# Value tile 6 moved from the end of the attention opening into the first group's planned order

## The reference

```
x = x + 0.5 * ffn_ref(layernorm(x), ...)      # attention, then a mixture of experts
x = x + attn_ref(layernorm(x), ...)           # RWKV time mix and channel mix
x = x + 0.5 * ffn_ref(layernorm(x), ...)

def attention(x, wq, wk, wv, wo):             # 16 query heads, 4 key/value heads of 128
    q, k, v = x @ wq, x @ wk, x @ wv          # then rotary embedding on q and k
    scores = q @ k.T / sqrt(128), causal
    return softmax(scores) @ v @ wo
def moe(x, gate_w, w1, w3, w2):               # 8 experts, 2 of them per token, softmax of the two logits
```

## Time and profile before

| | |
|---|---|
| time before, median of 3 runs | 1285.56 us (1282.88 to 1286.85) |
| the profiled execution | 1284.35 us, of it 1282.5 us from the first instruction to the last |
| TensorE busy | 1150.7 us, 90% of the span |
| VectorE busy | 951.0 us, 74% |
| ScalarE busy | 783.1 us, 61% |
| GpSimd busy | 600.0 us, 47% |

### The profile page before, as it was taken

The page is one execution under the profiler, slowest core; times in us unless marked ns, Lnnn a source line. Parts: engine busy times, 40 slices in busy tenths (PEclk is TensorE's granted clock), DMA queues, the critical chain, the costliest instruction groups (busy, mean ns, idle before and its releaser), DMA issues.

```text
span 1282.5 us, 18567 instructions
## 1 busy us (share of the span) xinstructions
PE 1150.7 (90%) x6424; PEld 965.5 (75%) x6424; DVE 951.0 (74%) x2013; ACT 783.1 (61%) x1542; POOL 600.0 (47%) x450
## 2 busy tenths in 40 slices
PE   4899999999999799953388789999999999989994
PEld 3688888888898488841277678888888888748883
DVE  6677887877886677748757667788788788677773
ACT  5666666666665477732453666666666666457772
POOL 3566666666610145522512356666665760014551
PEclk9999999999999899985779889999999999999997
DMA  4100100100015611134100200010010010651113
GB/s 133 38 1 1 38 1 1 38 1 2 10 41 197 228 43 50 54 96 134 54 1 1 70 1 1 1 38 1 1 38 1 1 50 1 231 197 50 50 54 119
DMA packets 48652, 66.29 MB, mean 52 GB/s; under 512 B 5808, under 2 KB 34352, under 8 KB 48432
## 3 DMA queue, kind: packets, MB, share of 16 engines
q1 hardware_dynamic: 42032, 50.94, 12.2%
q0 software_dynamic: 4416, 12.06, 3.1%
q10 hardware_dynamic: 2112, 2.10, 0.5%
HBM read 54.86 MB, written 10.22 MB: 51 GB/s over the span
## 4 chain that ended last, share of the span: by engine, by line
PE 80%; DVE 10%; ACT 4%; DMA 2%; issue 2%; POOL 2%; SPq 0%; DVEq 0%; ACTq 0%; POOLq 0%
PE ps L1456 20%; PE ps L1458 19%; PE ps L1457 19%; PE ps L1526 9%; PE ps L1607 6%; PE ps L1595 2%; PE ps L1420 1%; POOL probs L739 1%; DVE h L1153 1%; PE ps L1578 1%; DMA mixT<-y_dram 1%; DVE mixT L1385 1%; ACT probs L807 1%; DVE ps L1131 1%; PE ps L1555 1%
## 5 line engine op out<-in xcount | busy, mean ns | idle before, releaser
L807 ACT ACTIVATE probs<-ps,negmax 128x128 f32<-128x128 f32 (+7 forms) x256 | 189.9, 742 | 91.5 <-DVE negmax L1131 88.5
L813 ACT ACTIVATE probsT<-ps 128x512 fp32r<-128x512 f32 x288 | 170.5, 598 | 116.9 <-PE ps L1526 115.5
L1137 DVE TENSOR_TENSOR probsT<-ps,probsT 128x512 fp32r<-128x512 f32 x288 | 196.0, 685 | 51.4 <-ACT probsT L813 49.9
L1131 DVE CUSTOM_DVE_ANT_0 ps<-ps,causal 128x128 f32<-128x128 f32 (+7 forms) x256 | 193.3, 762 | 25.8 <-PE ps L1458 23.9
L663 POOL TENSOR_TENSOR crossed<-crossed,rope 128x512 f32<-128x512 f32 x70 | 90.8, 1298 | 194.9 <-ACT crossed L793 194.9
L1526 PE MATMUL ps<-square,probs 128*128 128x128 f32 x1152 | 171.0, 273 | 0.4 <-DVE probsT L1137 0.3
L1526 PEld LDWEIGHTS ps<-square,probs 128*128 128x128 f32 x1152 | 141.3, 140 | 29.8 <-DVE probsT L1137 1.6
L710 POOL DMA_INDIRECT xs<-rows_dram,token_of x46 | 68.5, 1489 | 184.8 <-DMA rows_dram<-probs 162.3
L1153 DVE SCALAR_TENSOR_TENSOR h<-ps,rowinv,h 128x256 f32<-128x256 f32 x256 | 123.6, 483 | 36.2 <-PE ps L1458 27.7
L1244 DVE TENSOR_TENSOR parts<-experts,parts 128x1024 fp32r<-128x1024 f32 x92 | 112.4, 1225 | 48.6 <-ACT parts L857 48.1
L1456 PE MATMUL ps<-keysT,queriesT 128*128 128x512 f32 (+4 forms) x384 | 141.8, 369 | 3.3 <-DVE straight L1107 1.4
(11 more groups left out here) (245 smaller groups left out, 2848.4 us busy)
## 6 DMA issues: line engine op xcount, KB each, us to landing
experts<-in_L_ffn_w_dram SPq DMA_DIRECT2D x48, 512.0 KB, 7.9
w_in<-in_L_ffn_wq_dram SPq DMA_DIRECT2D x8, 512.0 KB, 3.9
wo_in<-in_L_ffn_wo_dram SPq DMA_DIRECT2D x8, 512.0 KB, 5.9
rows_dram<-probs ACTq DMA_DIRECT2D x4, 512.0 KB, 8.1
probs<-y_dram SPq DMA_DIRECT2D x8, 256.0 KB, 4.1
mixT<-y_dram SPq DMA_DIRECT2D x8, 256.0 KB, 5.0
probs<-in_L_attn_x_dram SPq DMA_DIRECT2D x2, 512.0 KB, 4.5
w_in<-in_L_ffn_wk_dram SPq DMA_DIRECT2D x8, 128.0 KB, 5.0
```

Of the source, the lines that this page charges most:

```text
L807: act.activation(probs[:, i % 2, k, 0:w], ps[:, 2 * slot_n:2 * slot_n + 2, :].rearrange("p b n -> p (b n)")[:, at:at + w], ACT.Exp, bias=n ...
L813: act.activation(probsT[:, m % 3, 0, :], ps[:, 4 + m % 2, :], ACT.Copy).then_inc(S["probsT_high"], 1)
L1131: dve.tensor_tensor_reduce(out=row, in0=row, in1=causal[:, T - w:T], scale=-1.0, scalar=LARGEST, op0=ALU.add, op1=ALU.min, accum_out=negma ...
L1137: dve.tensor_tensor(probsT[:, m % 3, 1, :], ps[:, 4 + m % 2, :], probsT[:, m % 3, 0, :].bitcast(F32), ALU.subtract).then_inc(S["probsT_low ...
```

## The change

The opening no longer issues value tile 6 on TensorE. The planner places it instead: it may come at any place after turn(0, 0), which the last added argument says, and before the steps that need it. Tile 7 was and is placed by the planner (its "needs" now name tile 6 and turn(0, 0) too). ScalarE's and VectorE's shares of tile 6 were already in the planned part. The gate of the experts keeps working on the raw tokens h as before.

```diff
@@ -143,8 +143,8 @@
     if opening:
         for t in range(4, NT):
             place = t - 2.5 if t == NT - 1 else 0.1 + 0.25 * (t - 4)
-            if t == NT - 1:
-                add("PE", ("v", t, 0), 1.39, place)
+            if t >= 6:
+                add("PE", ("v", t, 0), 1.39, place, ("v", t - 1, 0), ("turn", 0, 0))
             add("ACT", ("v_high", t, 0), 0.6, place, ("v", t, 0), ("v_high", t - 1, 0))
             add("DVE", ("v_low", t, 0), 0.69, place, ("v_high", t, 0), ("v_low", t - 1, 0))
             for i in range(t, NT):
@@ -241,7 +241,7 @@
             pe += [("v", n - 2, 0)]
     for k in range(REP):
         pe += [("scores", i, k) for i in range(EARLY)]
-        pe += [("v", 3 + k, 0)]
+        pe += [("v", 3 + k, 0)] if k < REP - 1 else []
```

## The result

Seven runs of the changed kernel have a median of 1280.54 us (1275.67 to 1282.61), seven of the kernel before 1284.54 us (1282.88 to 1287.35). The two medians lie 4.0 us apart. The ratio of the fast runs, which is not formed from the medians, is 0.9960, 95% interval 0.9949 to 0.9972: 5.1 us less, between 3.6 and 6.6. Forecast were 3.6 us and 1281.9. With four more runs the median of before came down from 1285.56 to 1284.54, so 3.6 us off it would now be 1280.9.

What follows compares the result with a forecast made beforehand. TensorE, busy for 90% of the span, was taken as the bound. Order 2.4 us plus clock 1.2 us gave 3.6 us off 1285.56: 1281.9 us, own range 1280.8 to 1282.8, 8 in 10 1278.5 to 1285.3.

Steps and rivals of the forecast that it cites:

- The seam: TensorE after each opening's last scores: turn(0, 0) starts 1.21 us earlier than tile 6 did; stall 1.85 us, was about 3.06.
- No stall at tile 6's new place: TensorE behind project kk: tile 6's bank is already free, no wait; GpSimd's chain starts 2.6 to 4.0 us earlier.
- T0: Zero point of the forecast's hand replay: end of the opening's last exp on ScalarE, 44.41 us in the first attention.
- Rival 4: GpSimd's rotations do not start earlier and hold TensorE's gain to 1.3 us per attention: 1283.0 us; chance 0.05.
- The order behind the seam: TensorE from turn(0, 0) to scores(4, 3): gain by order 1.2 us per attention, 2.4 us in all.
- 2.9 us of short waits in either order: TensorE's short waits from the last exp to the stall ahead of scores(4, 0), 2.9 us in both orders by replay.
- Rival 3: VectorE can't feed the four "out" in their new places: 3.4 us of waits per attention, 1288.8 us; chance 0.08.
- The clock: Low clock behind both stalls cost 4.2 us before; 1.5 per opening, 3.0 in all, with the change; gain 1.2 us.
- Rival 2: Clock doesn't fall behind the shorter stall: one opening spared gives 1280.5 us, both 1279.0; chance 0.2.
- The sum: Order 2.4 us plus clock 1.2 us: 3.6 us less, 1281.9 us from the median of 1285.56.
- the range of 8 in 10: Forecast of the whole kernel's time, taking in rivals and the spread of runs: 1278.5 to 1285.3 us.

Runs made afterwards that it cites:

- Bank 5: Kernel before with tile 6 kept at its old place but put in bank 5 instead of bank 7; 1278.75 us, ratio 0.9952.
- the seam with fillers: Kernel before with only tile 6 moved behind project kk, plus 7 unread matmuls ahead of turn(0, 0); 1276.82 us, ratio 0.9938.
- the fillers: Kernel before with 12 extra matmuls, results unread, in the stall just ahead of tile 6; 1279.13 us, ratio 0.9961.
- the second profile: The changed kernel run and profiled once more, unedited; 1278.06 us, ratio 0.9960 against the kernel before.
- the seam alone: Kernel before with only tile 6's matmuls, copies and low part moved behind project kk's steps, all else in the old order; 1278.57 us, ratio 0.9952.
- kk first: Changed kernel with project kk moved ahead of turn(0, 0) on TensorE; 1278.52 us, ratio 0.9954 against the kernel before.

## Why the prediction was right

**The seam.** Right to 0.1 us. turn(0, 0) starts 1.93 us behind the last scores, released by the exp, where tile 6 had started after 3.06 (forecast: 1.85). Bank 5 shows the cause another way.

**No stall at tile 6's new place.** Right: no idle time ahead of 45.67, and GpSimd's chain started 2.9 us earlier against T0 (forecast 2.6 to 4.0), its cover rose to 2.2. Rival 4 is out.

**The order behind the seam.** The forecast saw the wait ahead of turn(2, 0) (0.9; it was 0.74), but had "2.9 us of short waits in either order". That term was mis-sized: the new order waits 0.3 us more per attention, as the seam with fillers shows (34.8 against 35.1). The gain by order is therefore 1.9 us, not 2.4. Rival 3's waits ahead of the four "out" did not come; what VectorE's longer list costs is 0.3 us by way of turn(2, 0), of the 3.4 us that the rival was priced at.

**The clock.** The price before, 4.2 us, was about right (3.9 by the fillers against the first profile, 4.3 over four profiles). With the change I took 1.5 per opening. Where the clock fell it cost 1.35 to 1.68; but in the second profile it stayed up in one of two openings, so 2.2 us on the mean of few, not 3.0, and the gain by the clock is about 2.0 instead of 1.2 (4.3 - 2.2, rounded; 1.7 if the price before is taken as 3.9). Rival 2, one opening spared, is true of some executions.

**The sum.** 1.9 + 2.0 = 3.9 us, shown by the stretches, for 3.6 forecast: two errors of opposite sign, 0.5 too much by order and 0.8 too little by the clock, nearly cancel. That the total came out so near is luck in part; the mechanism was right. The medians lie 4.0 us apart, which leaves nothing over. The ratio says 5.1 with 3.6 to 6.6 in its interval, which leaves about 1 us, and most of the other kernels too gained more by their ratio than by their stretches. The measured 1280.54 lies 0.3 us under the forecast's own range of 1280.8 to 1282.8, at the 1280.5 of rival 2 with one opening spared, and inside the range of 8 in 10.

Whether that last 1 us is real stays open. If it is, it lies between the attentions, which took 661.9 to 665.1 us in the four profiles of before and 660.6 to 663.2 in all others, while the second attention behind its opening is the same to 0.2 us in all of the table. Most of it is in the 180 matmuls matched above: 54.3 us on the mean of four before, 52.6 on the mean of two with the change, with less time at the low clock. That would be a second place where the clock costs less. No step of the forecast looked there, no edit touched that stage, and the first profile of before already has its short time there, so it is not shown that the change brings it about; chance in few profiles is a rival that stands.

## What to carry to other kernels

A step that waits for a buffer holds up all that is queued behind it on its engine. Ask of the longest stall which of the next steps could already run; here turn(0, 0) could, 1.1 us before tile 6. Better than moving the waiting step out of the stall is to give it a buffer that is free when the stall begins, so that it fills it: bank 5 gained 7.2 us in these stretches against the first profile of before, the move 3.1 and 4.1 in its two profiles.

To price the clock behind a stall, fill the stall with matmuls that nobody reads and measure the stretch behind it; a few tenths of a us that whole runs with a spread of 4 to 10 us can't tell are plain in such a stretch. It shows only its own part of the gain, though: compare the other stages too, by matching instructions.

## What was not expected of the hardware

The same stall in the same program does not always cost the same. Stalls of 3.05 us among dense matmuls came with the low clock, during them or within 1.6 us behind them, in 8 of 8 openings; stalls of 1.84 to 1.94 us in 6 of 8 (the change 3 of 4, the seam alone 1 of 2, kk first 2 of 2); stalls of 0.6 us in none of 4. In the second opening of before the clock was low for 6.8 us each time, in the first for 3.4 us in three profiles and 6.8 in one. The Trainium skill, "TensorE: Matmul & The Clock Gate", section on the clock gate, says that the low clock is the default and activity releases it; the trace agrees in that fillers with no use to the program, 12 of them in 2.76 us in each opening, kept the clock at 1.00 there and made it 5.0 us faster, 3.9 of them in the two openings.
